# Seven-product down projections, kept transposed, for the second pair of batches of an attention and expert kernel

## The reference

```python
x = x + attention(layernorm(x), ctx, ...)            # (4, 512, 512)
h = layernorm(x)
weights = router_weights(h, Wr, temperature)         # (b, t, e)
gate = einsum("btd,edf->ebtf", h, Wg)                # experts 0 and 1: + h Ga Gb
up   = einsum("btd,edf->ebtf", h, Wu)                # experts 0 and 1: + h Ua Ub
mid  = silu(gate) * up
out  = einsum("ebtf,efd->ebtd", mid, Wd)             # experts 0 and 1: + mid Da Db
x = x + einsum("bte,ebtd->btd", weights, out)
```

## Time and profile before

| | |
|---|---|
| median of 3 runs | 1055.22 us (1054.95 to 1056.51) |
| the profiled execution | 1055.69 us, its span 1054.0 us |
| PE busy | 1042.4 us, 99% |
| DVE busy | 708.8 us, 67% |
| ACT busy | 449.5 us, 43% |
| moved by DMA | 94.73 MB, mean 90 GB/s |
| granted TensorE clock | 1.000 |

### The profile page before, as it was taken

How to read it: one execution, slowest core, us unless ns; L and a number is a source line. 1 busy time by engine, 2 the same in 40 slices (tenths; PEclk the granted TensorE clock), 3 DMA queues, 4 the chain that set the end, 5 groups by cost and what they waited for, 6 DMA issues and landing times.

```text
span 1054.0 us, 12230 instructions
## 1 busy us (share of the span) xinstructions
PE 1042.4 (99%) x4680; PEld 853.0 (81%) x4680; DVE 708.8 (67%) x1212; ACT 449.5 (43%) x653; POOL 50.4 (5%) x62
## 2 busy tenths in 40 slices
PE   8999999999999999999999999999999999999998
PEld 5887787878888888888888888788888888888887
DVE  7878678877484866838487684847566473838544
ACT  4654363554442543444344344525334343524430
POOL 2511121100000000000000000000000000000000
PEclk9999999999999999999999999999999999999999
DMA  9410104334151322415135537202021121112012
GB/s 297 156 50 1 81 21 160 106 94 140 60 148 32 125 75 81 140 61 145 35 115 165 177 103 239 59 23 80 23 78 41 60 60 60 41 40 79 21 41 80
DMA packets 91307, 94.73 MB, mean 90 GB/s; under 512 B 4464, under 2 KB 67056, under 8 KB 90352
## 3 DMA queue, kind: packets, MB, share of 16 engines
q1 hardware_dynamic: 90096, 90.73, 27.4%
q0 software_dynamic: 864, 3.15, 1.0%
q10 hardware_dynamic: 288, 0.07, 0.0%
HBM read 76.63 MB, written 17.30 MB: 89 GB/s over the span
## 4 chain that ended last, share of the span: by engine, by line
PE 86%; DVE 8%; issue 2%; ACT 2%; DMA 1%; POOL 0%; SPq 0%; DVEq 0%
PE gate_up L1621 15%; PE gate_up L1623 15%; PE gate_up L1622 15%; PE tiles L1508 10%; PE tiles L1510 10%; PE tiles L1509 10%; PE gate_up L1579 2%; PE gate_up L1580 2%; PE gate_up L1585 2%; PE tiles L1544 1%; DVE piece_lo L1187 1%; DMA wd_raw<-in_wd_dram 1%; DVE mids_lo L1265 1%; DVE xacc L1239 1%; DVE tx_lo L1248 0%
## 5 line engine op out<-in xcount | busy, mean ns | idle before, releaser
L1621 PE MATMUL gate_up<-xT_hi,piece_hi 128*128 128x512 f32 x448 | 174.8, 390 | 1.0 <-DVE mids L1226 0.6
L1508 PE MATMUL tiles<-wd_hi,mids_hi 128*128 128x512 f32 x448 | 174.4, 389 | 0.4 <-DVE mids_lo L1265 0.4
L1623 PE MATMUL gate_up<-xT_lo,piece_hi 128*128 128x512 f32 x448 | 174.4, 389 | 0.0
L1622 PE MATMUL gate_up<-xT_hi,piece_lo 128*128 128x512 f32 x448 | 174.4, 389 | 0.0
L1509 PE MATMUL tiles<-wd_lo,mids_hi 128*128 128x512 f32 x448 | 174.3, 389 | 0.0
L1510 PE MATMUL tiles<-wd_hi,mids_lo 128*128 128x512 f32 x448 | 174.3, 389 | 0.0
L1239 DVE SCALAR_TENSOR_TENSOR xacc<-tiles,rw,xacc 128x512 f32<-128x512 f32 x112 | 78.0, 750 | 138.5 <-PE tiles L1510 138.5
L1187 DVE TENSOR_TENSOR piece_lo<-piece,piece_hi 128x1024 fp32r<-128x1024 f32 x112 | 118.2, 1097 | 28.9 <-ACT piece_hi L821 27.6
L1621 PE MATMUL gate_up<-tx_hi,piece_hi 128*128 128x512 f32 x336 | 130.9, 389 | 0.3 <-DVE gates L1216 0.3
L1622 PE MATMUL gate_up<-tx_hi,piece_lo 128*128 128x512 f32 x336 | 130.8, 389 | 0.0
L1623 PE MATMUL gate_up<-tx_lo,piece_hi 128*128 128x512 f32 x336 | 130.8, 389 | 0.0
(11 more groups left out here) (176 smaller groups left out, 1406.2 us busy)
## 6 DMA issues: line engine op xcount, KB each, us to landing
piece<-in_wg_dram SPq DMA_DIRECT2D x40, 256.0 KB, 3.2
piece<-in_wu_dram SPq DMA_DIRECT2D x40, 256.0 KB, 3.3
wd_raw<-in_wd_dram SPq DMA_DIRECT2D x10, 1024.0 KB, 5.3
piece<-merged SPq DMA_DIRECT2D x32, 256.0 KB, 3.3
merged<-lora_w SPq DMA_DIRECT2D x6, 1024.0 KB, 4.3
x_back<-x_spill SPq DMA_DIRECT2D x9, 512.0 KB, 5.3
wd_raw<-merged SPq DMA_DIRECT2D x4, 1024.0 KB, 5.6
out_dram<-xacc SPq DMA_DIRECT2D x16, 256.0 KB, 4.1
```

Source lines behind the costliest of these rows:

```text
L1508: nc.tensor.matmul(dst, w_h, x_h, start=first, stop=False)
L1621: nc.tensor.matmul(dst, w_h, x_h, start=first and kt == 0, stop=False, skip_group_check=True)
L1622: nc.tensor.matmul(dst, w_l, x_h, start=False, stop=False, skip_group_check=True)
L1623: ins = nc.tensor.matmul(dst, w_h, x_l, start=False, stop=last and kt == 1, skip_group_check=True)
```

## The change

Only steps 7 to 12 of the second pair change their down projections. They are now made by seven products too: a quarter of Wd is a piece like those of gate and up, the mids of both batches are the moving operand, and the result is transposed, output features by tokens. So the router's weights, which belong to tokens, are multiplied onto the gates beforehand (`scale_gates`, with the weights turned by one transpose in step 6, stored in DRAM and loaded as rows, `load_rw_rows`). DVE forms the four mixes of mids (`mix_of`), ACT and DVE split seven operands for each half (`operand_high_part`, `operand_low_part`, instead of four mids), and DVE adds the results in six operations a quad to `acc_t`, where the sum over the six experts stays transposed until step 13. There 32 transposes turn it back (`turn_back`) and DVE adds it to the running outputs (`add_turned_back`). Step 13 keeps the plain `down_half`.

PE's order of steps 8 to 13 is six quads: G0, G1, D0, D1 (the down pieces of step `k - 1`), U0, U1. The fourth of G1 is in D0, that of D0 in D1, that of D1 in U0.

The gate and up pieces of steps 1 to 5 (`n` = 4 to 23) are stored in DRAM by POOL when they are split, 2 x 917 KB each, and steps 8 to 12 load them back finished: no sums, no splits for these 20. Pieces of step 7, of step 13 and all down pieces are loaded raw. The diff, cut; its fragments are, in this order: the tables, the finished load, SP's steps 8 to 13, POOL's stores, four fragments of ACT's steps 8 to 13, DVE's first half of the operands, three fragments of DVE's steps 8 to 13, PE's steps 8 to 13:

```diff
+QUADS = [(k, which, m) for k in range(SWAP + 1) for which in (GATE, UP) for m in range(2)] \
+    + [(k - (which == DOWN), which, m) for k in range(SWAP + 1, STEPS) for which in (GATE, DOWN, UP) for m in range(2)]
+FINISHED = [which != DOWN and SWAP < k < STEPS - 1 for k, which, m in QUADS]
+FIRST_STORED, LAST_STORED = 4, 4 * (SWAP - 1)
...
+            def load_finished_piece(n):
+                k, which, m = QUADS[n]
+                for part, halves in enumerate(piece_halves(n)):
+                    sp.dma_start(halves, spilled(4 * (k - SWAP) + 2 * which + m, part)).then_inc(piece_back[n % 3], 16)
...
+            for k in range(SWAP + 1, STEPS):
+                last = k == STEPS - 1
+                if not last:
+                    sp.wait_ge(gates_scaled, 4 * (k - SWAP))
+                    load_rw_rows(k)
+                load_next_piece(NUMBER[k - 1, DOWN, 0])
+                load_next_piece(NUMBER[k - 1, DOWN, 1])
+                load_next_piece(NUMBER[k, UP, 0])
+                load_next_piece(NUMBER[k, UP, 1])
+                if last:
+                    sp.wait_ge(q_mm, q_done(6, 2 * (k - SWAP) - 1))
+                    load_wd(k)
+                    sp.wait_ge(q_mm, q_done(4, 2 * (k - SWAP) - 1))
+                    sp.dma_start(xacc[:, 2 * TT * D:], acc_spill).then_inc(acc_loaded, 16)
+                else:
+                    load_next_piece(NUMBER[k + 1, GATE, 0])
+                    load_next_piece(NUMBER[k + 1, GATE, 1])
...
+            for j in range(FIRST_STORED, LAST_STORED):
+                store_piece(j)
             load_again(0, 0, 1)
...
+                copy_p1(j)
+                operand_high_part(k - 1, 1, B11)
+                if last:
+                    piece_high_part(NUMBER[k, GATE, 1])
+                copy_p5(j)
...
+                copy_u2(j + 1)
+                piece_high_part(NUMBER[k - 1, DOWN, 0])
...
+                copy_q_u2(d)
+                piece_high_part(NUMBER[k - 1, DOWN, 1])
+                copy_q1(d + 1)
+                copy_q5(d + 1)
+                copy_q_u2(d + 1)
+                if last:
+                    piece_high_part(NUMBER[k, UP, 0])
...
+                    if k == STEPS - 2:
+                        piece_high_part(NUMBER[k + 1, GATE, 0])
+                    operands_of_first(k)
...
+            def operands_of_first(k):
+                combine(k, UP, 0, C12)
+                make_mid(k, 0, C12)
+                if k == STEPS - 2:
+                    piece_low_part(NUMBER[k + 1, GATE, 0])
+                combine(k, UP, 0, C22)
+                make_mid(k, 0, C11)
+                make_mid(k, 0, C22)
+                mix_of(k, 0, T1)
+                operand_low_part(k, 0, B11)
+                mix_of(k, 0, T2)
+                mix_of(k, 0, T3)
+                operand_low_part(k, 0, T1)
+                operand_low_part(k, 0, B22)
+                make_mid(k, 0, C21)
+                mix_of(k, 0, T4)
+                combine(k, UP, 1, C12)
+                make_mid(k, 1, C12)
+                operand_low_part(k, 0, T2)
+                operand_low_part(k, 0, T3)
+                operand_low_part(k, 0, B21)
+                operand_low_part(k, 0, T4)
...
+                combine(k - 1, UP, 1, C22)
+                make_mid(k - 1, 1, C11)
+                if last:
+                    piece_sums(NUMBER[k, GATE, 1])
+                mix_of(k - 1, 1, T1)
+                operand_low_part(k - 1, 1, B11)
+                make_mid(k - 1, 1, C22)
+                if last:
+                    piece_low_part(NUMBER[k, GATE, 1])
...
+                combine(k, GATE, 0, C12)
+                operand_low_part(k - 1, 1, T2)
+                operand_low_part(k - 1, 1, T3)
+                combine(k, GATE, 0, C22)
...
+                    combine(k, UP, 1, C22)
+                    add_turned_back(1)
...
+                quad(j, True)
+                quad(j + 1, True)
+                down_quad(d)
+                down_quad(d + 1)
+                quad(j + 2, False, d + 1)
+                if k == STEPS - 1:
+                    turn_back(0)
+                quad(j + 3, True)
```

More of the change, by code:

```diff
@@ L485, in _ @@
             store_merged(0)
-            for k in range(1, STEPS):
+            for k in range(1, SWAP + 1):
                 if k < len(LORA_JOBS):
@@ L868, in _ @@
             act.wait_ge(x_stored, 64)
-            for k in range(STEPS):
+            def operands_of_first(k):
+                j = 4 * k
+                copy_p1(j + 3)
+                operand_high_part(k, 0, B11)
+                copy_p5(j + 3)
+                operand_high_part(k, 0, T1)
+                operand_high_part(k, 0, B22)
+                operand_high_part(k, 0, T2)
+                operand_high_part(k, 0, T3)
+                copy_u2(j + 3)
+                operand_high_part(k, 0, B21)
+                operand_high_part(k, 0, T4)
+            for k in range(SWAP + 1):
                 j = 4 * k
@@ L1417, in _ @@
                     combine(k, GATE, 1, C22)
-                    combine(k, UP, 0, C12)
+                    scale_gates(k, 0)
+                    scale_gates(k, 1)
+                    operands_of_first(k)
+                    break
                 elif k > 0:
@@ L1502, in _ @@
+            add_down(STEPS - 1, 0)
+            add_down(STEPS - 1, 1)
         @block.tensor
@@ L1628, in fourth, with down_product @@
                 product(j, 4, gate_bank(j), last=True)
-            def quad(j, pending):
+            def down_product(d, i, dst, first=False, last=False):
+                n = NUMBER[SWAP + d // 2, DOWN, d % 2]
+                hi, lo = piece_hi[n % 3], piece_lo[n % 3]
+                pe.wait_ge(operand_ready, 14 * (d // 2) + 7 + OPERAND[i] + 1)
+                for kt in range(2):
+                    cols = slice(kt * P, (kt + 1) * P)
+                    w_h, w_l = hi[:, COMBO[i] - 1, cols], lo[:, COMBO[i], cols]
+                    raw, x_h, x_l = operand_of(OPERAND[i], kt)
+                    nc.tensor.matmul(dst, w_h, x_h, start=first and kt == 0, stop=False, skip_group_check=True)
+                    nc.tensor.matmul(dst, w_l, x_h, start=False, stop=False, skip_group_check=True)
+                    ins = nc.tensor.matmul(dst, w_h, x_l, start=False, stop=last and kt == 1, skip_group_check=True)
+                ins.then_inc(q_mm, 1)
@@ L1632, in quad @@
+            def quad(j, pending, down_pending=None):
                 k = j // 4
```

441 lines of the change are left out of this document (387 added, 54 removed).

## The result

The changed kernel takes 1058.66 us (median of 9 runs, 1058.41 to 1059.28); the kernel before took 1055.70 beside it (9 runs). The ratio is 1.0029, 95% interval 1.0018 to 1.0039: slower by 0.3%, 1.3 us above the forecast of 1057.4 and inside its range. The profiled execution took 1058.47 us with a span of 1056.7 (before 1054.0), at a granted clock of 1.00.

The account below looks back on a forecast made before the run. The prediction took TensorE, busy 99% of the span, as the bound, so only matmul count and late operands mattered. Its terms summed to +2.2 us, from a median of 1055.2 to 1057.4 us, range 1048 to 1065.

Parts of the forecast that it names:

- transposes: 32 transposes turning the sums back, in two bursts of 16, and one for the router weights, on TensorE: +3.7 us.
- 13 raw quarters: D0 and D1 of six steps and U0 of step 13: operand 0.44 us late, 0.62 us each, +8.1 us.
- end of step 12: G0 of step 13 is raw again, so C22 of U0 is done at 52.0, wanted at 50.32: +1.9 us.
- start of step 13: VectorE free late, G1's split ahead of copy_p5, late combines C22 of U1, C12 and C22 of G0: +3.8 us.
- last turn: Step 13: add_turned_back waits for the acc load, and down_half(13, 0) for the first add of add_turned_back(1): +2.0 us.
- swap step: Waits behind a late p5 copy and a late mid, 0.5 us each, go with the raw piece's sums and splits: -1.0 us.
- first rival: Steps 12 and 13 hide their lateness; only matmuls, transposes and the 13 pieces count: -5.5, 1049.7 us; chance 0.18.
- the second: Rival: the raw pieces are on time too, so their waits cost nothing: -13.6, 1041.6 us; chance 0.07.
- VectorE in steady steps: Steps 8 to 12: VectorE has 41.5 of 57.1 us of work, slack 0.6 at two places a step: cost 0.
- third rival: VectorE decides steady steps 8 to 12, losing about 0.7 at each of two places a step: +7, 1064 us; chance 0.17.
- The loads and the stores: Finished pieces land in 7 to 11 us, cost 0 up to 14.8; POOL's stores in steps 1 to 5 cost nothing.
- fourth rival: Stores crowd the loads: wd late by 4 us delays copy_p1 in each of five steps, +12.5, 1070 us; chance 0.10.

## Why the prediction was right

The sum came out by its own terms. By the starts of TensorE's matmuls, each gap less 0.2267, and the 0.1 of the next one added:

| term | predicted | measured |
|---|---|---|
| 72 matmuls | -16.3 | -16.3 (4680 to 4641, with 33 transposes) |
| transposes | +3.7 | +3.7 (two bursts of 1.67 and 0.09 behind each, the single one 0.2) |
| 13 raw quarters | +8.1 | +7.8 (13 x 0.60) |
| end of step 12 | +1.9 | +1.9 (1.76 + 0.11) |
| start of step 13 | +3.8 | +3.6 (1.15, 1.5, 0.6, 0.3) |
| last turn | +2.0 | +2.2 (0.46 and 1.78) |
| swap step | -1.0 | -1.0 (both waits gone) |
| sum | +2.2 | +1.9 |

The span grew by 2.7. Of the missing 0.8 us, 0.3 are there by step 7's first half (the wait of the earlier trace rows comes at 617.12 instead of 616.84), 0.2 of them by the end of step 0's first wait; the rest is spread in amounts of 0.1 us and less, as in steps 8 to 11, 58.35 to 58.44 long where 252 matmuls and two waits give 58.3. The median rose by another 0.3 (3.0 against 2.7). The forecast started from 1055.2, and the longer series gave 1055.7 for the same kernel: that accounts for 0.5 of the 1.3 us by which the result lies above it. What moves between executions of one kernel is as large as these remainders, so they are not evidence for or against a term.

**The raw quarters.** Right in place, number and size: the operand was 0.44 us late, as forecast, and a wait cost 0.60 where 0.62 was taken. It is shown by the two kernels that move the split one place each way: -7.8 when it goes ahead, +13.1 for six when it goes back.

**End of step 12 and start of step 13.** Right, and shown by finishing those two quarters: the waits go with the sums and splits. The first rival, that the end is hidden, is refuted: steps 12 and 13 lost 7.7 us, far from the 3.4 at which the sign would have turned. So is the second.

**VectorE in steady steps.** No wait for a combine shows in steps 8 to 11, and none appears when the subtractions are moved ahead. The third rival is refuted here. The slack at the two places can be read in the changed kernel. In step 9 the combine for C22 of U1 ends at 728.09 and the product that needs it starts at 728.68; for C22 of G0 it is 737.48 and 738.20. So 0.59 and 0.72 us were left, where I had 0.6 at both.

```profile
727.41 0.68 DVE L1451 TENSOR_TENSOR mids<-p_sb,gate_up 128x512 f32<-128x512 f32 x1
```

```profile
728.68 0.39 PE L2039 MATMUL gate_up<-tx_hi,piece_hi 128*128 128x512 f32 x1
```

**The transposes.** Right, 0.11 us each; the doubling shows it.

**The loads and the stores.** The two parts of a finished quarter landed 4.5 and 6.4 us after issue, under the 7 to 11 that I took, and nothing waited for them. The stores cost 0, as I took it, but the reason I gave was too easy: I looked at SP's slot wait and the wd load, and argued from mean traffic (97 of about 400 GB/s). What the stores really delay is two other things. One is the merged weight's write, from 4.3 us to 6.1 at the median of six, and behind it SP's queue, and behind that ScalarE's. The other is any quarter load issued beside them: the two at 252.42 and 252.83 landed in 7.2 and 7.5 us, before the change in 2.9 and 3.3, which nobody waited for. At the place shown above 2.0 us of 6.2 of cover were used up, all by the write. The fourth rival, which I gave 0.10 and put at the wd load, named the right resource at the wrong load. It did not happen, by 4.3 us, and nothing in the prediction had measured that margin: this term was right for a reason that was not its own.

**A reading.** The prediction calls TensorE's last waits "all under 0.4 us"; the one of the earlier trace rows is 0.43. Nothing rests on it.

## What to carry to other kernels

A product that is removed pays only as far as the operand of the next one is there earlier too: 16.3 us of matmuls were taken out, and 15.5 us came back as waits. The orders of two queues made 10.0 of them, and the sums and splits of two raw quarters at the end the other 5.5. Put what the next product needs ahead of what merely empties a bank, on each engine in the chain. And cover is to be measured at the load with the least of it, by doubling the suspect, not by mean traffic: stores that cost nothing once cost 47 us twice.

## What the runs showed of the hardware

A matmul held up by a late operand is followed by a loss of 0.08 to 0.11 us at the next matmul, at every such wait of steps 0 to 13 that left the clock up.

A transfer's landing depends on what is issued beside it: the two loads of 256 KB for one quarter took 6.2 and 6.4 us when no store was issued just before them, and 14.2 and 15.5 us beside four stores of 896 KB.
